# Attention: where the row maxima are turned, and how many steps the keys run behind the scores

## The reference, cut to what matters

```python
q = (layernorm(x) @ Wq + bq)   # -> [batch, head, 1024, 32]
k = (ctx @ Wk + bk)            # -> [batch, head, 2048, 32]
v = (ctx @ Wv + bv)
attn = clip(q @ k.T * 32 ** -0.5, -1e4, 1e4)
attn = softmax(attn)
x = x + tanh(g_xattn) * ((attn @ v) @ Wo + bo)
x = x + tanh(g_ffn) * ffn(layernorm(x))     # 512 -> 2048 -> 512, silu
```

## Time and profile before

| | |
|---|---|
| median of 3 runs | 3244.92 us (3243.12 to 3249.04) |
| the profiled execution | 3243.34 us, its span 3241.5 us |
| attention | about 477 to 2346 us of the span |
| PE busy / VectorE / ScalarE / GpSimd | 3105.8 / 1977.7 / 1560.6 / 1867.2 us |

### The profile page before, as it was taken

One profiled execution on the slowest core, in us unless ns is written; L12 is line 12 of the kernel. 1 busy time (PEld: TensorE's weight loads), 2 busy tenths in 40 slices (PEclk: granted clock), 3 DMA queues, 4 the chain that ended last, 5 costly groups with the idle time before them and its releaser, 6 DMA issues. The chain is left out here.

```text
span 3241.5 us, 51516 instructions
## 1 busy us (share of the span) xinstructions
PE 3105.8 (96%) x15973; PEld 1901.5 (59%) x15973; DVE 1977.7 (61%) x2795; ACT 1560.6 (48%) x2851; POOL 1867.2 (58%) x889
## 2 busy tenths in 40 slices
PE   6799979999999999999999999999878999999999
PEld 5588854444444444444444444444355888878887
DVE  8766657766667666666666666766566733333332
ACT  2222216767666676667776676766612311111111
POOL 4656537888888888888888888888741000000000
PEclk9899989999999999999999999999988999999999
DMA  4556674221222212222122221222096000000000
GB/s 164 205 192 213 221 229 98 60 55 43 59 59 59 56 43 57 59 59 58 43 56 59 59 58 46 53 59 59 23 283 223 1 26 27 27 27 26 26 14 13
DMA packets 139907, 258.82 MB, mean 80 GB/s; under 512 B 16946, under 2 KB 57906, under 8 KB 132532
## 3 DMA queue, kind: packets, MB, share of 16 engines
q1 hardware_dynamic: 139156, 249.37, 27.3%
q10 hardware_dynamic: 672, 8.39, 0.8%
HBM read 166.48 MB, written 91.23 MB: 80 GB/s over the span
## 5 line engine op out<-in xcount | busy, mean ns | idle before, releaser
L892 DVE TENSOR_REDUCE at_half_max<-ps 128x1 f32<-128x1024 f32 x1024 | 1210.1, 1221 | 555.5 <-PE ps L707 548.6
L638 POOL TENSOR_TENSOR at_gp_sum<-at_gp_sum,at_probT 128x1024 f32<-128x1024 f32 x512 | 1218.7, 2380 | 42.2
L830 ACT ACTIVATE at_probT<-ps 128x512 f32<-128x512 f32 x2048 | 1071.0, 600 | 160.2 <-PE ps L726 139.2
L707 PE MATMUL ps<-at_k_stack,at_q_stack 96*128 96x512 f32 x2048 | 876.9, 430 | 28.0 <-DMA at_k_stack<-kT_hi 19.3
L726 PE MATMUL ps<-at_q_stack,at_k_stack 98*128 98x512 f32 x2048 | 808.4, 396 | 1.4 <-ACT at_probT L830 1.1
L707 PEld LDWEIGHTS ps<-at_k_stack,at_q_stack 96*128 96x128 f32 x2048 | 389.7, 191 | 466.0 <-DVE at_half_max L892 382.4
L765 PE MATMUL ps<-at_probT,at_v_head 128*32 128x512 f32 x4096 | 492.5, 598 | 0.9 <-ACT at_probT L830 0.9
L633 POOL TENSOR_TENSOR at_gp_sum<-at_probT 128x1024 f32<-128x1024 f32 x128 | 304.5, 2379 | 316.9 <-ACT at_probT L830 316.9
L726 PEld LDWEIGHTS ps<-at_q_stack,at_k_stack 98*128 98x128 f32 x2048 | 390.0, 191 | 70.2 <-ACT at_probT L830 7.1
L1444 POOL TENSOR_TENSOR x_keep<-x_keep,b_half 128x2048 f32<-128x2048 f32 x8 | 37.6, 4706 | 613.7 <-DVE x_keep L1467 613.7
L1423 ACT ACTIVATE ff_y<-ps,b_t 128x512 f32<-128x512 f32 x128 | 88.1, 688 | 578.0 <-PE ps L1379 577.9
(11 more groups left out here) (174 smaller groups left out, 3804.7 us busy)
## 6 DMA issues: line engine op xcount, KB each, us to landing
at_k_stack<-kT_hi SPq DMA_DIRECT2D x128, 256.0 KB, 4.9
kT_hi<-kv_k_hi SPq DMA_DIRECT2D x16, 1024.0 KB, 4.2
kT_lo<-kv_k_lo SPq DMA_DIRECT2D x16, 1024.0 KB, 6.5
v_heads<-kv_v_out SPq DMA_DIRECT2D x16, 1024.0 KB, 5.7
at_q_stack<-qT_hi SPq DMA_DIRECT2D x128, 128.0 KB, 3.3
at_k_stack<-kT_lo SPq DMA_DIRECT2D x64, 256.0 KB, 4.3
at_v_head<-v_heads SPq DMA_DIRECT2D x64, 256.0 KB, 5.1
kv_c_in<-in_ctx_dram SPq DMA_DIRECT2D x16, 768.0 KB, 7.1
```

What stands on the lines that cost most here:

```text
L638: pool.tensor_tensor(gp_sum[lane % 2][:, :, :], gp_sum[lane % 2][:, :, :], pairs[:, 2 * i + 2:2 * i + 4, :], ALU.add).then_inc(gp_added, 1)
L707: mm = pe.matmul(ps[:, n, :], q_stack[buf][0:PARTS, rows], k_stack[buf][0:PARTS, BANK * n:BANK * (n + 1)], start=True, stop=True)
L830: act.activation(probT[lane % 2][:, kv, :], src, ACT.Exp).then_inc(exp_done, 1)
L892: dve.tensor_reduce(dst, src, AX_X, ALU.max).then_inc(max_done, 1)
```

## The change

The four identity matmuls and ScalarE's copy leave the path that runs. VectorE writes the high and low parts of minus the maxima side by side into columns 0 to 3 and 4 to 7 of a tile `neg` of 128 x 32, and turns that tile in its four 32 x 32 blocks (`transpose`). After that block g holds in its first 8 partitions the two parts of four groups of 32 queries. SP copies each block's 8 x 32 numbers into rows 96 and 97 of q_stack with one DMA, four a unit, on the chip from one on-chip memory place to another. KEYS goes from 6 to 7 and PV, SUMS and FOLD by one as well. The first key tile waits for the four DMAs, and the ring of banks no longer has a place for the turned maxima. In the clipping path the turn stays.

```diff
-    TURN, KEYS, PV, SUMS, FOLD = 5, 6, (9, 10), 11, 12
+    TURN, KEYS, PV, SUMS, FOLD = 6, 7, (10, 11), 12, 13
 def key_bank(lane, kv):
-        return 4 + ((KVT + 1) * lane + kv + 1 + (kv >= KVT - 2)) % RING
+        return 4 + (KVT * lane + kv) % RING
+            def lay_out_maxima(head, slot, half):
+                unit = HALVES * head + half
+                sp.wait_ge(split_done, SPLITS * (unit + 1))
+                rows = q_stack[slot][PARTS:PARTS + 2, BANK * half:BANK * (half + 1)].bitcast(F32) \
+                    .rearrange("w (t g r) -> w t g r", t=QT, g=P // D)
+                for g in range(P // D):
+                    block = turned[half][D * g:D * g + 2 * QT, :]
+                    sp.dma_start(rows[:, :, g, :], block).then_inc(row_loaded, 16)
             def step(base, slot):                       # SP, one step a head
                 ... loads of head n into its slot ...
+                if (n := at(base, slot, 2, BUFS, N_HEADS)) is not None:
+                    lay_out_maxima(n, (slot - 2) % BUFS, 1)
                 ... stores of head n - 3 ...
+                if (n := at(base, slot, 1, BUFS, N_HEADS)) is not None:
+                    lay_out_maxima(n, (slot - 1) % BUFS, 0)
 def keys(base, slot, i):
                 if kv == 0:
-                    pe.wait_ge(row_copied, unit + 1)
-                if kv:
-                    need(pe, exp_done, KVT * unit + kv - 2 + (kv >= KVT - 2))
+                    pe.wait_ge(row_loaded, 64 * (unit + 1))
+                need(pe, exp_done, KVT * unit + kv - RING + 1)
-            def turn_maxima(base, slot):     # PE, now in the clipping path alone
-                    else:
-                        mm = pe.matmul(ps[0:2, bank, cols], neg_hi[:, t, :], ident_r[:, :],
-                                       start=True, stop=True)
 def split_maxima(base, slot):                # VectorE
-                    dve.tensor_reduce(neg_hi[:, :, 1], neg_lo[:, :, :], AX_X, ALU.max).then_inc(split_done, 1)
+                    dve.tensor_reduce(neg[:, QT:2 * QT], neg_lo[:, :, :], AX_X, ALU.max).then_inc(split_done, 1)
+                dve.wait_ge(split_done, n + 5)
+                need(dve, row_loaded, 64 * (unit - 1))
+                dve.transpose(turned[half][:, :], neg[:, :].bitcast(F32)).then_inc(split_done, 1)
```

More of the change, by code:

```diff
@@ L541, in attend @@
     KVT = SK // P
-    TURN, KEYS, PV, SUMS, FOLD = 5, 6, (9, 10), 11, 12
+    TURN, KEYS, PV, SUMS, FOLD = 6, 7, (10, 11), 12, 13
     TAIL = FOLD + 1 - QT
     RING = 3
+    SPLITS = 6
     GP_ADDS = 5
@@ L576, in attend @@
         neg_lo = sb("neg_lo", [P, QT, 1])
-        neg_hi = sb("neg_hi", [P, QT, 2], F32R)
+        neg = sb("neg", [P, D], F32R)
+        turned = [sb(f"turned{i}", [P, D]) for i in range(HALVES)]
         partial = sb("partial", [P, BANK])
@@ L595, in attend @@
         split_done = sem("split_done")
+        row_loaded = sem("row_loaded")
         row_turned = sem("row_turned")
@@ L682, in load_early_sums @@
                     sp.wait_ge(stored[half], 64 * EARLY)
-                sp.wait_ge(const, 3 + 2 * BUFS)
+                sp.wait_ge(const, 4 + 2 * BUFS)
                 sp.wait_ge(max_done, 2 * STEPS)
@@ L689, in _ @@
             run_steps(sp, step, N_HEADS, BUFS, first=2, tail=BUFS)
+            sp.wait_ge(row_loaded, 64 * UNITS)
             for half in range(HALVES):
@@ L719, in keys @@
                 if kv == 0:
-                    pe.wait_ge(row_copied, unit + 1)
-                if kv:
-                    need(pe, exp_done, KVT * unit + kv - 2 + (kv >= KVT - 2))
+                    pe.wait_ge(row_loaded, 64 * (unit + 1))
+                    if clipping:
+                        pe.wait_ge(row_copied, unit + 1)
+                need(pe, exp_done, KVT * unit + kv - RING + 1)
                 q = BANK * (lane % HALVES)
@@ L728, in keys, with spread_maxima @@
                           start=True, stop=True).then_inc(tile_done, 1)
-            def turn_maxima(base, slot):
+            def spread_maxima(base, slot):
                 unit, lane, r = unit_at(base, slot, TURN)
-                if unit is None or r:
+                if unit is None or r or not clipping:
                     return
-                pe.wait_ge(split_done, 5 * (unit + 1))
-                need(pe, exp_done, KVT * unit - 4)
-                bank = turn_bank(lane)
+                pe.wait_ge(split_done, SPLITS * (unit + 1))
+                need(pe, gather_done, unit - 1)
                 for t in range(QT):
                     cols = slice(P * t, P * (t + 1))
[L741 to L745, removed]
-                    else:
-                        mm = pe.matmul(ps[0:2, bank, cols], neg_hi[:, t, :], ident_r[:, :],
-                                       start=True, stop=True)
+                    for part in range(2):
+                        mm = pe.matmul(ps[:, 7, cols], wide[:, part, t, :], ident_r[:, :],
+                                       start=(part == 0), stop=(part == 1))
                 mm.then_inc(row_turned, 1)
@@ L762, in values @@
                     need(pe, gather_done, unit)
+                    if clipping and not (isinstance(unit, int) and unit + 1 >= UNITS):
+                        pe.wait_ge(row_copied, unit + 2)
                 for r in rounds:
@@ L796, in step @@
                 keys(base, slot, 1)
+                spread_maxima(base, slot)
                 values(base, slot, PV[0], (0, 1))
@@ L800, in step @@
                 last_sums(base, slot)
-                turn_maxima(base, slot)
                 scores(base, slot, 2)
@@ L810, in _ @@
         def _(pe):
-            pe.wait_ge(const, 3 + 2 * BUFS)
+            pe.wait_ge(const, 4 + 2 * BUFS)
             by_path(pe, pe_steps)
@@ L833, in copy_maxima @@
                 unit, lane, r = unit_at(base, slot, TURN)
-                if unit is None or r:
+                if unit is None or r or not clipping:
                     return
                 act.wait_ge(row_turned, unit + 1)
[L837 to L843, removed]
+                need(act, shift_done, KVT * (unit - 1))
+                act.copy(neg_rows[lane % 2][:, :], ps[:, 7, :]).then_inc(row_copied, 1)
             def copy_partial(base, slot):
@@ L898, in split_maxima @@
                 unit, first = BODY * base + slot // QT, slot - (QT - 1)
-                n = 5
+                n = SPLITS * unit
+                half = slot // QT % HALVES
                 pair = half_max[:, first:first + QT, :]
                 dve.wait_ge(max_done, 2 * QT * (unit + 1))
-                need(dve, split_done, n * unit)
+                need(dve, split_done, n)
                 if clipping:
@@ L905, in split_maxima @@
                                              ALU.max, ALU.max).then_inc(split_done, 1)
-                    dve.wait_ge(split_done, n * unit + 1)
+                    dve.wait_ge(split_done, n + 1)
                     need(dve, row_turned, unit)
-                    dve.tensor_scalar(neg_hi[:, :, 0], row_max[:, :], -1.0, None, ALU.mult).then_inc(split_done, 1)
-                    dve.wait_ge(split_done, n * unit + 2)
-                    dve.scalar_tensor_tensor(neg_hi[:, :, 1], row_max[:, :], -1.0, neg_hi[:, :, 0].bitcast(F32),
+                    dve.tensor_scalar(neg[:, 0:QT], row_max[:, :], -1.0, None, ALU.mult).then_inc(split_done, 1)
+                    dve.wait_ge(split_done, n + 2)
+                    dve.scalar_tensor_tensor(neg[:, QT:2 * QT], row_max[:, :], -1.0, neg[:, 0:QT].bitcast(F32),
                                              ALU.mult, ALU.subtract).then_inc(split_done, 1)
-                    dve.wait_ge(split_done, n * unit + 3)
+                    dve.wait_ge(split_done, n + 3)
                     for part in range(2):
-                        dve.tensor_copy(wide[:, part, :, :], neg_hi[:, :, part:part + 1].bitcast(F32)
+                        dve.tensor_copy(wide[:, part, :, :], neg[:, QT * part:QT * (part + 1)].bitcast(F32).unsqueeze(2)
                                         .to_broadcast([P, QT, P])).then_inc(split_done, 1)
@@ L918, in split_maxima @@
                     dve.tensor_reduce(neg_pair[:, :, 1].bitcast(F32R), pair, AX_X, ALU.max).then_inc(split_done, 1)
-                    need(dve, row_turned, unit)
-                    dve.tensor_reduce(neg_hi[:, :, 0], pair, AX_X, ALU.max, negate=True).then_inc(split_done, 1)
-                    dve.wait_ge(split_done, n * unit + 2)
+                    dve.tensor_reduce(neg[:, 0:QT], pair, AX_X, ALU.max, negate=True).then_inc(split_done, 1)
+                    dve.wait_ge(split_done, n + 2)
                     dve.tensor_reduce(neg_lo[:, :, 0], neg_pair[:, :, :], AX_X, ALU.add).then_inc(split_done, 1)
-                    dve.wait_ge(split_done, n * unit + 4)
-                    dve.tensor_reduce(neg_hi[:, :, 1], neg_lo[:, :, :], AX_X, ALU.max).then_inc(split_done, 1)
+                    dve.wait_ge(split_done, n + 4)
```

(7 more changed lines are left out.)

4 lines of the change are left out of this document (1 added, 3 removed).

## The result

The changed kernel takes 3264.31 us (median of 4 runs, 3261.82 to 3264.42) against 3244.62 us: ratio 1.0059, 95% interval 1.0047 to 1.0072, so 19.7 us slower. The forecast was 3267 us. The profiled execution took 3261.82 us (span 3259.7), 18.5 us above that of before.

What follows compares the result with a forecast made beforehand. TensorE was taken as the bound, already waiting once a unit for VectorE's reductions and maxima. 3243.34 + 13.9 (loop) + 8.7 (start and tail) = 3265.9; the median lies 1.6 us higher: 3267 us, range 3245 to 3295.

Steps and rivals of the forecast that it cites:

- The chain on VectorE: Small reductions, then maxima that scores 0 awaits: waits and transpose inserted in series add 0.30 us a unit, 38.4 us.
- Rival (c): VectorE's transpose waits 1.0 us on average for a port shared with GpSimd, TensorE after it: 3393 us; chance 0.04.
- The turn's gain: Four turn matmuls leaving TensorE's stream save 0.19 us a unit, 24.3 us, not the 0.41 of their row.
- The gap: TensorE's interval ahead of scores 0, two steps after the split, grows from 0.36 to about 0.66 us.
- The DMAs in the loop: Four small DMAs a unit land before the key tile that needs them, even behind a head's loads: cost 0.
- rival (b): Small DMAs land late in the loop too, in units behind the loads; 3 us give 3460 us; chance 0.05.
- 4 us of cover: In the loop, small DMAs land by about 21.5, the key tile needs them at about 26: some 4 us spare.
- The start: First key tile waits for unit 0's small DMAs, from 495.7 to 502.9; ninth step +6.0, plus 0.6 for the clock.
- The order that the forecast took: At the start, unit 0's small DMAs queue behind head 1's loads, landing at 501.9, and land at about 502.9.
- The 0.6 that the forecast added for the clock: At the start, 0.6 us added because TensorE's clock comes up later.
- The tail: One step of keys, four tiles, moves behind the last scores, where ScalarE sets the pace: +2.1 us.
- the standstill of 0.13: TensorE already stands still 0.13 us ahead of scores 0, once a unit, waiting for VectorE's chain; grows to 0.43.

Runs made afterwards that it cites:

- e3: Changed kernel with only the transpose and its two waits one step later on VectorE, the small reductions left in place: 3228.55 us, ratio 0.9945.
- e1: Changed kernel with the split and transpose of a unit's maxima one step later on VectorE, behind the next unit's first row maxima: 3191.53 us, ratio 0.9830.
- e2: Kernel before, turn still on TensorE, with only the split of the maxima one step later on VectorE: 3211.34 us, ratio 0.9894.
- e5: Changed kernel with the old lags, one step less between split and keys (KEYS 6, PV 9 and 10, SUMS 11, FOLD 12): 3265.37 us, ratio 1.0062.
- e6: Changed kernel with ScalarE's two 4 MB feed-forward weight loads issued only after head 1's queries and keys have landed: 3266.73 us, ratio 1.0069.
- e8: Changed kernel with ScalarE's two 4 MB feed-forward weight loads issued at step 516, in the attention's tail: 3264.21 us, ratio 1.0064.

## Why the prediction was right

**The chain on VectorE** was taken from the rows of before, instruction by instruction, and came out at +0.33 for +0.30: the pair of waits cost what it had cost ahead of line 917, and the transpose held the engine 0.14 us for 0.12. e3 shows that it is this chain. The page of the Trainium skill on the ways to transpose (VectorE: DVE Perf Modes, "The three transpose paths") gives durations, 390 ns on TensorE and 311 ns on VectorE for bf16. Ranked by durations alone the change would have been a gain. The trace agrees with the ranking: the row of the transpose is 0.21 us long and that of the four matmuls 0.41. Yet what counts is 0.33 in series on one engine against about 0.2 in the stream of the other. Rival (c), a wait for GpSimd, did not happen: 128 transposes took 0.211 to 0.214 us each, beside additions that fill most of the time.

```profile
L934 DVE STREAM_TRANSPOSE at_turned<-at_neg x128: 211/213/214, 487.9 to 2336.8; 128x32 f32<-128x32 f32 x128
```

**The turn's gain** was 0.18 to 0.21 us a unit (e3 against the kernel before, e1 against e2) and not the 0.41 of its row. **The gap** grew from 0.36 to 0.66 as forecast; why 0.30 of the chain's 0.33 reach TensorE is not shown. In the loop the forecast was 13.9 us and 14 were measured.

**The DMAs in the loop** were covered, as forecast, and rival (b) fell. The forecast's 4 us of cover fit e5, where 3.1 us less of it still left no wait.

**The start** is the term that was sized too high: 6.6 us in the forecast, 3.5 measured. The hole began at 495.15 (forecast 495.7) and ended at 499.79 (forecast 502.9), and the ninth step began at 502.95 (forecast 506.0). The order that the forecast took, small DMAs behind head 1's loads, is what the changed kernel shows: they let the tile start 0.1 us behind the landing of head 1's values. That landing came 2.2 us earlier than in the rows of before (0.4 by the issue, 1.8 by a landing time of 34.2 and not 36.0), and the small DMAs came 0.1 and not 1.0 behind it. What the forecast did not see is why head 1's loads took so long. It is the weights' transfer on ScalarE's queue, without which they take 8.9 us (e6) and the hole is gone (e8), and which holds the small DMAs by itself when SP's queue is empty (e6). The 0.6 that the forecast added for the clock was not measured apart. **The tail** was 2.6 for 2.1. Start and tail together were 6.1 for 8.7.

**The number** is closer than these terms. The profiled execution took 3261.8 us where 3265.9 were forecast: 2.6 of the 4.1 are start and tail, and 1.2 the earlier first scores, which are no part of the change. The median then lay 2.5 us above the profiled execution and not 1.6, so that 3264.3 comes nearer to 3267 by luck.

**Unsaid by the forecast:** that the chain was a loss of 0.30 us a unit in the kernel before, and so a gain of 34 us with no other change (e2). It read the standstill of 0.13 in one unit; in every sixth unit, at the loop's end, it is 0.52, and each standstill carries 0.10 more behind it. That part is equal before and after within 0.02 us, so it did not touch the difference.

## What to carry to other kernels

Moving work off the busiest engine gains what it costs in that engine's stream, and loses all that it adds to a chain the busiest engine already waits for, even where the other engine is only 61% busy. Before moving work there, look for the engine's slack at another place in its own order: the same operations one step later were worth 73 us here, almost three times what the turn had cost TensorE (0.61 against 0.21 us a unit). A small transfer that something waits for lands late while a large transfer of another queue is on the way; moving the large one helps only if nothing else pays for it, and in e8 the next phase did.

## What the runs showed of the hardware

- A VectorE transpose of 128 x 32 float32 lasts 0.20 to 0.21 us, its successor starts 0.12 to 0.14 behind its start, and beside GpSimd's additions, which fill 82% of the time in the loop, none lasts longer.
- A standstill of TensorE between two 512-column matmuls costs 0.10 us beyond its idle time: the next matmul follows 0.33 to 0.34 us behind instead of 0.23 (changed kernel against e1).
- Four DMAs of 1 KB from one on-chip place to another take SP 2.6 to 3.0 us to issue, 0.61 each. At the start of the changed kernel, with head 1's loads still under way in SP's own queue, they took 6.6; full DMA engines alone do not do that (share 1.08 in e6 from 486 to 489, where they took 2.8). The last lands within 2.7 us in the loop, but is used some 14 us after its issue beside a transfer of 4 MB in pieces of 32 KB from another queue (e6: issued by 488.9, used at 502.66).
